# Layer norm of the second and third attention moved from VectorE to GpSimd

## The reference

```
def ln(x, g, b, eps): mu = mean(x); var = mean((x - mu)**2)
                      return (x - mu) * rsqrt(var + eps) * g + b
x = ln(attention(x, ctx, side bias, key mask) + x, L0 gains, 1e-6)
x = ln(x + attention(x, x, pair mask), ln1_g, ln1_b, 1e-5)     # "second", stage SA
x = ln(x + attention(x, ctx),          ln2_g, ln2_b, 1e-5)     # "third",  stage CA
x = ln(x + relu(x @ W1.T + b1) @ W2.T + b2, ln3_g, ln3_b, 1e-5)
```

## Time and profile before

| what | us |
|---|---|
| median of 3 runs | 4732.81 (4731.19 to 4740.78) |
| the profiled execution, its own time | 4732.95 |
| its span in the trace | 4731.2 |
| first MAX of SA to first MAX of CA | 1698.9 to 2840.0 |
| one batch inside SA, first MAX to first MAX | 136.2 to 137.1 (typical) |
| one batch inside CA | 139.8 to 140.3 (typical) |
| share of the span in which each engine is busy | PE 91%, DVE 73%, ACT 58%, POOL 31% |

### The profile page before, as it was taken

How to read it: one execution, slowest core, us unless ns; L and a number is a source line. 1 busy time by engine, 2 the same in 40 slices (tenths; PEclk the granted TensorE clock), 3 DMA queues, 4 the chain that set the end, 5 groups by cost and what they waited for, 6 DMA issues and landing times. The chain is left out here.

```text
span 4731.2 us, 78898 instructions
## 1 busy us (share of the span) xinstructions
PE 4292.4 (91%) x23168; PEld 3461.4 (73%) x23168; DVE 3458.7 (73%) x7128; ACT 2765.7 (58%) x5985; POOL 1483.9 (31%) x1640
## 2 busy tenths in 40 slices
PE   7999998899999879999999969999999995999998
PEld 6888786777778657777777747777776774888887
DVE  6776776677887768888888868888889886333333
ACT  5655665555566557777777758777777774111111
POOL 2222221222332234444444424444444442010011
PEclk9999999999999989999999989999999998999999
DMA  2211111211111110000000020000011103010010
GB/s 89 70 47 51 62 62 70 77 47 47 51 62 53 49 55 27 19 23 27 27 27 14 23 87 19 26 30 25 29 36 36 36 10 118 12 42 31 31 44 32
DMA packets 110830, 203.66 MB, mean 43 GB/s; under 512 B 12416, under 2 KB 12416, under 8 KB 110592
## 3 DMA queue, kind: packets, MB, share of 16 engines
q1 hardware_dynamic: 110592, 201.13, 12.7%
HBM read 159.14 MB, written 41.94 MB: 43 GB/s over the span
## 5 line engine op out<-in xcount | busy, mean ns | idle before, releaser
L1283 POOL TENSOR_SCALAR QS<-QK 32x1024 fp32r<-32x1024 f32 (+2 forms) x1152 | 1172.0, 1017 | 2031.6 <-DVE QK L1031 1236.7
L870 ACT ACTIVATE R<-psT 128x512 fp32r<-128x512 f32 x1536 | 917.6, 597 | 966.4 <-PE psT L664 946.7
L863 ACT ACTIVATE PR<-PR,MN 128x512 f32<-128x512 f32 x1536 | 1104.5, 719 | 73.6 <-DVE MN L1016 39.9
L1088 DVE TENSOR_TENSOR R<-psT,R 128x512 fp32r<-128x512 f32 x1536 | 1049.2, 683 | 23.7 <-ACT R L870 21.3
L664 PE MATMUL psT<-ID,PR 128*128 128x128 f32 x6144 | 939.0, 276 | 72.7 <-DVE R L1088 57.3
L1016 DVE CUSTOM_DVE_ANT_0 PR<-psS,RAW 128x512 f32<-128x512 f32 x1024 | 700.0, 684 | 382.1 <-PE psS L643 274.2
L664 PEld LDWEIGHTS psT<-ID,PR 128*128 128x128 f32 x6144 | 746.8, 142 | 252.8 <-DVE R L1088 72.2
L685 PE MATMUL psV<-R 128*64 128x512 f32 (+1 forms) x3072 | 873.0, 407 | 42.6 <-DVE OG L1044 40.8
L685 PEld LDWEIGHTS psV<-R 128*64 128x64 f32 (+1 forms) x3072 | 468.7, 157 | 260.1 <-issue 34.7
L646 PE MATMUL psS<-QS 128*128 128x512 f32 x1024 | 499.5, 488 | 67.8 <-POOL QS L1283 41.5
L912 ACT ACTIVATE PR<-psS,COLS 128x512 f32<-128x512 f32 x128 | 88.3, 690 | 566.8 <-PE psS L598 566.8
(11 more groups left out here) (106 smaller groups left out, 8024.6 us busy)
## 6 DMA issues: line engine op xcount, KB each, us to landing
RAW<-in_w SPq DMA_DIRECT2D x96, 256.0 KB, 4.4
RAW<-in_ctx_t SPq DMA_DIRECT2D x96, 256.0 KB, 2.8
x<-Y SPq DMA_DIRECT2D x96, 256.0 KB, 2.0
RAW<-x SPq DMA_DIRECT2D x96, 256.0 KB, 2.7
Y<-x SPq DMA_DIRECT2D x96, 256.0 KB, 3.8
RAW<-in_x SPq DMA_DIRECT2D x64, 256.0 KB, 2.9
RAW<-in_side SPq DMA_DIRECT2D x64, 256.0 KB, 2.6
Y<-in_x SPq DMA_DIRECT2D x32, 256.0 KB, 3.9
```

Source lines behind the costliest of these rows:

```text
L863: nc.scalar.activation(prob(st, k), prob(st, k), ACT.Exp, bias=MN[:, k % 8:k % 8 + 1], scale=-1.0, accum_out=row_sums(st, SM, g)[:, qt, j: ...
L870: nc.scalar.activation(PT[h % 2][:, 0, :, qt * P:(qt + 1) * P], turned(place[k]).rearrange("p (k t) -> p k t", k=NT), ACT.Copy).then_inc(t ...
L1088: nc.vector.tensor_tensor(lo, turned(place[k]).rearrange("p (k t) -> p k t", k=NT), f32(hi), ALU.subtract).then_inc(t_evac, 1)
L1283: nc.gpsimd.tensor_scalar(to, pair, 1.0, 1.0, ALU.mult, ALU.mult).then_inc(stacked, 1)
```

## The change

In SA and CA (st.dk == 32) the two VectorE operations L980 and L984 are replaced by three GpSimd operations in three steps of the timetable: NORM (centre: subtract the mean and multiply by rstd, both as per-partition columns), NORM_GAIN (times the gain row) and NORM_BIAS (plus the bias row). They stand in slots 17, 18, 19 for the first tile and three slots later for each further one, and the last tile has them in slots 26, 27, 28. STORE comes one slot later than before (21, 24, 27, 30). L0b and FF keep the two VectorE operations. The core of the diff:

```diff
+        if wide:
+            add(out + step + 4, "NORM", tt)
+            add(out + step + 5, "STORE", tt)
+        else:
+            add(out + step + 3, "NORM", tt)
+            add(out + step + 4, "NORM_GAIN", tt)
+            add(out + step + 5, "NORM_BIAS", tt)
+            add(out + step + 7, "STORE", tt)
...
+            def centre(tt):
+                settle(False)
+                pool.wait_ge(rstd, tal["rstd"].done(tal["rstd"].marked(tt)))
+                gate()
+                issued("scaled")
+                tal["scaled"].mark(tt)
+                nc.gpsimd.tensor_scalar(Y[:, tt], Y[:, tt], MV[:, tt, 0:1], RD[:, tt:tt + 1], ALU.subtract,
+                                        ALU.mult).then_inc(y_scaled, 1)
+
+            def gain(tt):
...
+                pool.wait_ge(y_scaled, tal["scaled"].done(tal["scaled"].marked(tt)))
...
+                nc.gpsimd.tensor_tensor(Y[:, tt], Y[:, tt], ROWS[:, 1], ALU.mult).then_inc(pool_gained, 1)
+
+            def offset(tt):
...
+                pool.wait_ge(pool_gained, tal["pool_gain"].done(tal["pool_gain"].marked(tt)))
...
+                nc.gpsimd.tensor_tensor(Y[:, tt], Y[:, tt], ROWS[:, 2], ALU.add).then_inc(y_done, 1)
```

More of the change, by code:

```diff
@@ L73 @@
     "VAR",
-    "NORM",
+    "NORM", "NORM_GAIN", "NORM_BIAS",
     "ROWMASK",
@@ L355, in build @@
         y_gain = sem("y_gain")
+        y_scaled = sem("y_scaled")
         y_done = sem("y_done")
+        pool_gained = sem("pool_gained")
         y_sum = sem("y_sum")
@@ L381, in counts @@
                         j_hi=2 * NG + NT, stack=H, pieces=3 * H, mask=1, mask_ready=1, side=NT, side_ready=NT, res=NT, y=NT, mv=NT,
-                        var=NT, rstd=NT, y_norm=NT, gain=NT, y_done=NT, y_sum=NT)
+                        var=NT, rstd=NT, y_norm=NT, scaled=NT, gain=NT, pool_gain=NT, bias=NT, y_done=NT, y_sum=NT)
         def turned(place):
@@ L430, in stage_loop @@
             names = names + (["mask", "mask_ready", "side", "side_ready"] if st.bias == "side" else [])
-            names = names + (["mv", "var", "rstd", "gain", "y_sum", "y_done"] if st.norm else [])
+            names = names + (["mv", "var", "rstd", "y_sum", "y_done"] if st.norm else [])
+            names = names + ((["gain", "bias"] if st.dk == 64 else ["scaled", "pool_gain", "bias"]) if st.norm else [])
             names = names + (["res"] if st.cols != "ZERO" else [])
@@ L1124, in run @@
                         elif step == "NORM":
-                            if st.norm:
+                            if st.norm and st.dk == 32:
+                                tal["rstd"].next()
+                                tal["mv"].next()
+                            elif st.norm:
                                 normalise(k)
@@ L1204, in _ @@
                        j=Tally(j_evac, credit=2), s=Tally(s_full), spread=Tally(r_spread), t=Tally(t_full), pieces=Tally(stacked),
-                       res=Tally(res_ready), rstd=Tally(rstd))
+                       res=Tally(res_ready), rstd=Tally(rstd), scaled=Tally(y_scaled), pool_gain=Tally(pool_gained), bias=Tally(y_done))
             last_op = [None]
             def settle(shifts):
-                sems = dict(spread=r_spread, pieces=stacked, res=res_ready, rstd=rstd)
+                sems = dict(spread=r_spread, pieces=stacked, res=res_ready, rstd=rstd, scaled=y_scaled,
+                            pool_gain=pool_gained, bias=y_done)
                 if last_op[0] and (shifts or last_op[0] == "pieces"):
@@ L1313, in run @@
                             deviation(k, st.eps)
+                        elif step == "NORM" and st.norm and st.dk == 32:
+                            centre(k)
+                        elif step == "NORM_GAIN":
+                            gain(k)
+                        elif step == "NORM_BIAS":
+                            offset(k)
+                        elif step == "STORE" and st.norm and st.dk == 64:
+                            tal["bias"].next()
                 stage_loop(pool, tal, st, ["recip", "j", "s", "spread", "t", "pieces"] + (["y"] if st.cols != "ZERO" else []), run)
```

10 lines of the change are left out of this document (8 added, 2 removed).

## The result

| | before | after |
|---|---|---|
| median, us | 4733.94 (4731.19 to 4740.78, 4 runs) | 4765.86 (4763.73 to 4769.27, 4 runs) |
| ratio, 95% interval | 1 | 1.0066 (1.0048 to 1.0083) |
| span of the profiled execution | 4731.2 | 4767.4 |
| VectorE busy, whole span | 3458.7 | 3359.9 |
| GpSimd busy, whole span | 1483.9 | 1776.6 |

The account below looks back on a forecast made before the run. TensorE and VectorE lie close together; which one ends a slot is read slot by slot. Span 4731.2 - 66.7 (VectorE's gain) + 12.6 (two drains) = 4677.1, with 1.75 outside the span 4678.9; forecast 4679 us, range 4665 to 4700.

Parts of the forecast that it names:

- The stall of TURN in slot 23: TensorE waits 2.47 us for a P_LO behind VectorE's second-tile norm; claimed to go but for 0.07, gaining 2.4 a batch.
- its low clock: Half clock for 3.4 us behind the slot 23 stall; claimed to stay up, gaining 1.44 us a batch (bounds 0 and 1.44).
- the wait of SCORE 32: TensorE waits 0.92 us (CA 0.77) for head 8's pieces; claimed to go, gaining 0.85 (CA 0.7) a batch.
- VectorE's gain, 66.7 us: Norms leaving VectorE in SA and CA: 4.84 us a batch in SA, 4.69 in CA, times seven each.
- Centre, 0.65 us within 0.65 and 1.319: GpSimd's subtract-and-multiply step, four a batch, priced at 0.65 us from rows with one wide input; upper end 1.319.
- d: How much longer GpSimd's work in a batch is than forecast; change worth zero at 2.5 us.
- the worst case I wrote down: Centre at its upper bound and the eight other GpSimd operations 0.3 us longer: d = 5.1, 4774 us; chance 0.07.
- The third rival: GpSimd becomes the bound at head 8's first piece, clock falls, drains grow: 4736 or 4774 us, chance 0.07 each.
- The formula: Price if GpSimd's work is d longer: 14 x (-4.8 + d - 0.4 + 1.44) + 12.6 + 2d.
- The second rival: Half clock moves to three later stalls in each SA batch, 30 us over seven batches: 4709 us; chance 0.15.
- The drains, 6.3 us each: Ends of SA and CA: longer GpSimd chain (17.5 us) delays stores and weight loads, 6.3 us each, bounds 5 to 9.
- Contention in the bodies: VectorE beside GpSimd's new work: only GROUP_LO, with two SBUF inputs, slows, by 0.6 us, covered by slack in slots 26, 27.

Follow-up runs that it names:

- e8: Changed kernel, only tiles 0 and 1 of the bodies on GpSimd; the rest and drains on VectorE, tile 3's norm in slot 31: 4678.3 us (0.9883).
- e11: Changed kernel, centre as multiply then add, drains on VectorE, tile 3 of the bodies on VectorE in slot 31: 4668.04 us (0.9871).
- e14: Kernel before, nothing on GpSimd; body norms on VectorE moved to slots 25, 41, 57, 63: 4689.31 us (0.9898).
- e17: The same kernel as e15, measured again: 4650.53 us (0.9847).
- e7: Changed kernel, gain step cut to the first column of 512, centre kept at 2.08 us: 4678.11 us (0.9884).
- e12: Kernel before, VectorE's norm of the second tile in SA and CA cut to one column, nothing put on GpSimd: 4697.61 us (0.9928).
- e9: Changed kernel, centre as multiply then add, with a small GpSimd operation making the extra column: 4703.48 us (0.9938).
- e1: Changed kernel, both column operands of centre replaced by immediates 0.0 and 1.0: 4746.06 us (1.0027).
- e10: Changed kernel, centre as multiply then add, norms of both drains on VectorE: 4674.33 us (0.9877).
- e15: Changed kernel, bodies' tiles 0 and 1 on GpSimd with multiply-add centre, tiles 2 and 3 on VectorE in slots 41, 57, drains on VectorE: 4656.18 us (0.984).

## Why the prediction was wrong

**What bounds the kernel: right.** The stall of TURN in slot 23, its low clock and the wait of SCORE 32 were the three things in reach, and slot 23 is free of idle time and at clock 1.00 in the kernel after. The wait of SCORE 32 did not go as told: it grew to 2.96 us with the low clock behind it, by the step below, and went only in e8, e11 and e14 to e17.

**VectorE's gain, 66.7 us: right in size, 69.7 in e7, in part by luck.** The stall and its clock were sized 0.6 to 0.7 us a batch too low and the share of SCORE 32 0.4 to 1.0 too high, as e7 shows. The sum holds for the norms taken off together. e12 shows that a part of it hangs on the rest: with only the stall gone 0.68 us a batch return at SCORE 32. The half clock's 1.44 us was real: slots 22 to 26 are 3.1 us shorter in e12, of which the stall's 1.68 are one part.

**Centre, 0.65 us within 0.65 and 1.319: the step that failed.** I wrote "Centre isn't in the trace; its nearest rows are L1308 ... and L1239" and called the second the upper bound. Both ends rested on counting wide inputs. The form, minus then times, was in no row of the trace, and all tensor_scalar rows on GpSimd there (pieces and SPREAD) were times 1.0 times 1.0. It measured 2.08 us (shown by the row of L1272, and by e7 and e9 to be what the time hangs on), so d is 4 x 1.43 = 5.7 us a batch, beyond the 5.1 of the worst case I wrote down, and the work "just fits, with some 0.4 us to spare" no longer. The sum hung on 0.4 us of slack and on an unmeasured operation with four copies a batch, and this rival had 0.14.

**The third rival was the mechanism.** Place (the pieces of head 8), sign, the low clock falling there and the drains growing are as told. The formula with d = 5.7 gives 14 x (-4.8 + 5.7 - 0.4 + 1.44) + 12.6 + 11.4 = 51 us; measured 36 in span. The drains are right (24 against 26.8), the bodies too high (27 against 11.8): lateness is spread over two waits, 0.90 at SCORE 28 and 2.96 at SCORE 32, 3.86 and not 5.3. That the first wait also makes K late, for which the rest would have waited anyway, is my reading; no run shows it alone. As a price the formula is poor: with d = 5.1 (e1) it gives 41 us, and 13 came. The zero of the formula at d = 2.5 (4 x 0.63) would be a centre of 1.27 us.

**The second rival, low clock at the later stalls,** did not decide here, but other runs have it. In SA the low clock fell at the end of three batches before and in e7, and of seven in e9 and e10, where slots 0 to 8 of a batch then take 1 us more. My "about two of three" for CA was high: it fell behind 11 of 20 such stalls, nearer one of two.

**The drains, 6.3 us each: right path, wrong length.** 13.2 and 13.6 measured. The chain is 7.2 us longer than the 17.5 forecast: 5.7 are centre's length, and some 2.8 came as a centre of 3.55 us (1.5 over the others), a gain of 1.83 (0.5 over) and a slower VAR (0.8 over) beside VectorE's splits of the new weights (below), which the sum left out; shorter waits and slightly shorter gain and bias steps took about 1.2 back. With the work shortened to the forecast's length (e7) they are 6.9 and 6.8.

**Contention in the bodies: right.** P_LO and MAX keep their 0.68 us beside centre, gain and bias (MAX: median 682 ns before and after), and GROUP_LO is charged as I had it, 0.6 taken, 0.7 measured:

```profile
2290.25 1.46 DVE L1072 SCALAR_TENSOR_TENSOR OT<-OG,COLS,OT 128x512 fp32r<-128x512 f32 x1
```

The Trainium skill (SBUF — State Buffer, "Who interferes with whom") says that a VectorE instruction with two SBUF inputs contends with a GpSimd instruction that reads SBUF. The traces agree, and in both directions: GROUP_LO goes from 0.75 to 1.46 us, and GpSimd's centre from 2.08 to 3.55 beside the splits. I had used the rule for VectorE alone and not for GpSimd in the drain.

**One wide input and two.** The Trainium skill (GPSIMD Engine Reference, "Engine selection") puts elementwise work on VectorE, and calls GpSimd about twice as slow with two inputs and near line rate with one. The verdict came true for this change. The figure for two inputs is near what the rows have, 1.30 us against VectorE's 0.75. The one for one input is true of the fast pairs alone, 0.62 us: with one wide input GpSimd took up to 1.95 us by the pair of operations and 2.08 with columns. There the measurement decides. And e15 shows that moving two tiles pays where nobody waits for GpSimd.

## What to carry to other kernels

Before work goes to another engine, look whether the exact operation, with its pair of arithmetic operations, has a row on that engine. If it has none, the nearest row is no bound, and a plan whose slack is 0.4 us with four such operations in a batch should be priced with a run of that operation first, or laid out so that nobody waits for it. The same work in other slots of its own engine gave more than half of the gain, with one slot of the four badly chosen; the best order moved only the two tiles that were in the way and left the drain alone, where each microsecond counts whole. And when a forecast's total comes true, compare the terms too: in e7 two of them were wrong in opposite directions.
